# The third layer's expert steps, cut from 23 steps of 128 rows to 20 steps of two half blocks of 64 rows

## The reference, cut to what matters

```python
router_logits = x @ gate_weight.T                       # 1024 x 8
probs = softmax(router_logits); top_v, top_i = top_k(probs, 2)
top_v = top_v / top_v.sum(-1)
for each expert e:                                      # gate_up 1024 x 256, down 256 x 512
    gate, up = split(x @ gate_up[e].T)                  # 512 + 512 columns
    y_e = (silu(gate) * up) @ down[e].T                 # 256 columns
    out += weight_of_e_for_each_token * y_e
```

## Time and profile before

| | |
|---|---|
| median of 3 runs | 457.62 us |
| the three runs | 454.16, 457.62 and 458.86 us |
| span of the profiled execution | 455.4 us (its own device time is not given apart from the three runs) |
| PE busy | 407.7 us, 90% |
| first to last step of the third layer | from 249.21 us to 394.82 us of the span |

### The profile page before, as it was taken

The page is one execution under the profiler, slowest core; times in us unless marked ns, Lnnn a source line. Parts: engine busy times, 40 slices in busy tenths (PEclk is TensorE's granted clock), DMA queues, the critical chain, the costliest instruction groups (busy, mean ns, idle before and its releaser), DMA issues.

```text
span 455.4 us, 6054 instructions
## 1 busy us (share of the span) xinstructions
PE 407.7 (90%) x1749; PEld 265.4 (58%) x1749; DVE 328.5 (72%) x620; ACT 239.2 (53%) x478; POOL 253.2 (56%) x352
## 2 busy tenths in 40 slices
PE   7798999999899989957967999999999999976895
PEld 7576787555455545535753455566655566653554
DVE  5998789999999999799874466557546311038994
ACT  6533682667667667579853233232333232339883
POOL 5474037676879996137506457856864553214641
PEclk9999999999999999989965999999999999999998
DMA  7900006456555645000115987898898885050011
GB/s 230 411 11 0 1 1 221 138 185 224 184 158 191 212 163 184 1 1 2 39 55 178 376 299 280 304 374 299 305 361 300 285 317 192 35 184 1 23 35 37
DMA packets 23665, 77.39 MB, mean 170 GB/s; under 512 B 3441, under 2 KB 7921, under 8 KB 20177
## 3 DMA queue, kind: packets, MB, share of 16 engines
q1 hardware_dynamic: 20336, 69.94, 43.5%
q0 software_dynamic: 2208, 6.03, 4.1%
q10 hardware_dynamic: 1088, 1.05, 0.7%
HBM read 71.76 MB, written 5.24 MB: 169 GB/s over the span
## 4 chain that ended last, share of the span: by engine, by line
PE 50%; DVE 28%; issue 12%; ACT 3%; POOL 3%; DMA 3%; SPq 0%; DVEq 0%; POOLq 0%; ACTq 0%
PE bank L1993 18%; PE bank L2013 10%; PE bank L1770 5%; DVE hx L1295 4%; DVE fw L1084 4%; DVE bw L1087 3%; PE bank L1615 3%; PE bank L1617 2%; PE bank L1616 2%; DVE fw L1092 2%; PE bank L2004 2%; DVE xp L1353 2%; PE bank L1692 2%; DVE gl L1574 2%; PE bank L1839 1%
## 5 line engine op out<-in xcount | busy, mean ns | idle before, releaser
L1993 PE MATMUL bank<-gu,xbT 128*128 128x512 f32 x184 | 84.6, 603 | 0.9 <-ACT xbT L920 0.9
L1770 PE MATMUL bank<-hx,w2raw 128*128 128x512 f32 x128 | 67.3, 607 | 4.6 <-DVE hx L1295 3.7
L1510 DVE TENSOR_TENSOR hm<-bank,sl 128x512 f32<-128x512 f32 x23 | 15.9, 692 | 69.3 <-PE bank L1993 37.9
L808 ACT ACTIVATE rl<-bank 128x512 f32<-128x512 f32 x64 | 38.1, 595 | 38.6 <-PE bank L1617 37.8
L1993 PEld LDWEIGHTS bank<-gu,xbT 128*128 128x128 f32 x184 | 35.2, 194 | 36.3 <-issue 33.8
L1615 PE MATMUL bank<-xlhi,w1hi 128*128 128x512 f32 x64 | 49.4, 771 | 0.0
L2013 PE MATMUL bank<-dn,hT 128*128 128x256 f32 x184 | 45.2, 389 | 3.4 <-ACT hT L931 0.8
L589 POOL DMA_INDIRECT y_rows<-yb,dest_i x23 | 25.0, 1088 | 35.4 <-ACT yb L937 34.8
L1295 DVE TENSOR_TENSOR hx<-bank,cwb 128x512 f32<-128x512 f32 x64 | 42.1, 660 | 3.1 <-ACT bank L812 3.1
L2013 PEld LDWEIGHTS bank<-dn,hT 128*128 128x128 f32 x184 | 33.1, 190 | 11.8 <-issue 8.2
L1092 DVE RECIPROCAL fw<-fw 128x256 f32<-128x256 f32 x23 | 39.8, 1732 | 0.0
(11 more groups left out here) (305 smaller groups left out, 931.7 us busy)
## 6 DMA issues: line engine op xcount, KB each, us to landing
gu<-in_gu SPq DMA_DIRECT2D x22, 1024.0 KB, 7.6
cwb<-cw_rows SPq DMA_DIRECT2D x32, 512.0 KB, 4.1
dn<-in_dn SPq DMA_DIRECT2D x23, 512.0 KB, 4.5
traw<-in_t SPq DMA_DIRECT2D x3, 1024.0 KB, 7.5
w1raw<-in_w SPq DMA_DIRECT2D x8, 256.0 KB, 4.9
w2raw<-in_w SPq DMA_DIRECT2D x8, 256.0 KB, 4.6
kT<-in_kt SPq DMA_DIRECT2D x4, 256.0 KB, 4.5
x<-in_x SPq DMA_DIRECT2D x2, 512.0 KB, 6.4
```

What stands on the lines that cost most here:

```text
L808: act.activation(rl[:, u % 3, :], bank[u % 4][:], ACT.Relu).then_inc(sem("r_ready"), 1)
L1770: pe.matmul(bank[4 + s][:], w2raw[:, e // 4 % 2, e % 4, :], hx[:, 0, u % 4, :], start=(e == 0), stop=(e == E0 - 1), skip_group_check=True) ...
L1993: ins = pe.matmul(bank[2 * (b % 2) + up][:], xbT[:, b % 2, k, :], gu[:, b % RING, k, up * I2:up * I2 + I2], start=(k == 0), stop=(k == KC ...
```

## The change

A step now holds two half blocks of 64 rows, numbers 2b and 2b+1, each with an expert of its own. Experts get whole half blocks, of which 2048 pairs can need 39, so there are 20 steps. In gate_up and down each matmul becomes two: the first has the lower 64 columns of the stationary tile and writes PSUM partitions 0 to 63, the second the upper 64 and partitions 64 to 127, each with its own weights moving. `gu` and `dn` hold four buffers, two for each half, taken by the parity of b. A buffer is loaded again only if its new owner differs from the expert that it held two steps before; the DMA that is not needed is started with a false condition. All four buffers are first filled with expert 0 ahead of the routing. The waits on SP become: gate_up(b-2) done for `gu`, down(b-2) done for `dn`.

```diff
-NB = (TOP2 * TOK + E2 * (P - 1)) // P
-NBW = 24
+PART = 64
+GROUPS = P // PART
+NB = -(-((TOP2 * TOK + E2 * (PART - 1)) // PART) // GROUPS)
+NH = GROUPS * NB
+FULL = TOK // PART
+FIRST = [0] * GROUPS
...
-        gu = sb("gu", [P, RING, KC, 2 * I2])
-        dn = sb("dn", [P, RING, I2 // P, C])
+        gu = sb("gu", [P, 2 * GROUPS, KC, 2 * I2])
+        dn = sb("dn", [P, 2 * GROUPS, I2 // P, C])
...
+        def part(g):
+
+            return slice(PART * g, PART * g + PART)
...
             sp.dma_start(rtraw[:], rt_d).then_inc(sem("rt_in"), 16)
+            for slot in range(2 * GROUPS):
+                e = FIRST[slot // 2]
+                sp.dma_start(gu[:, slot, :, :], gu_d[e, :, :, :]).then_inc(sem(f"gu_in{slot % 2}"), 16)
+                sp.dma_start(dn[:, slot, :, :], dn_d[e, :, :, :]).then_inc(sem(f"dn_in{slot % 2}"), 16)
...
+            def owners(b):
+
+                for g in range(GROUPS):
+                    h = GROUPS * b + g
+                    owner[h] = sp.value_load(owner_i[h:h + 1, 0:1], min_val=0, max_val=E2 - 1)
+
+            def held(b, g):
+
+                return owner[GROUPS * (b - 2) + g] if b >= 2 else FIRST[g]
+
             def up_weights(b):
 
-                e = sp.value_load(owner_i[b:b + 1, 0:1], min_val=0, max_val=E2 - 1)
-                wait(sp, sem("up_done"), b - RING + 1)
-                sp.dma_start(gu[:, b % RING, :, :], gu_d[bass.ds(e, 1), :, :, :].rearrange("o p k n -> p (o k) n")
-                             ).then_inc(sem(f"gu_in{b % RING}"), 16)
...
+                wait(sp, sem("up_done"), b - 1)
+                if b < 2:
+                    sp.wait_ge(sem(f"gu_in{b}"), 16 * GROUPS)
+                for g in range(GROUPS):
+                    e, slot = owner[GROUPS * b + g], 2 * g + b % 2
+                    sp.dma_start(gu[:, slot, :, :], gu_d[bass.ds(e, 1), :, :, :].rearrange("o p k n -> p (o k) n"),
+                                 cond=e != held(b, g)).then_inc(sem(f"gu_in{slot % 2}"), 16)
 
             def down_weights(b):
 
-                e = sp.value_load(owner_i[b:b + 1, 0:1], min_val=0, max_val=E2 - 1)
-                wait(sp, sem("d_done"), b - RING + 1)
-                sp.dma_start(dn[:, b % RING, :, :], dn_d[bass.ds(e, 1), :, :, :].rearrange("o p k n -> p (o k) n")
-                             ).then_inc(sem(f"dn_in{b % RING}"), 16)
-
+                wait(sp, sem("d_done"), b - 1)
+                if b < 2:
+                    sp.wait_ge(sem(f"dn_in{b}"), 16 * GROUPS)
+                for g in range(GROUPS):
+                    e, slot = owner[GROUPS * b + g], 2 * g + b % 2
+                    sp.dma_start(dn[:, slot, :, :], dn_d[bass.ds(e, 1), :, :, :].rearrange("o p k n -> p (o k) n"),
+                                 cond=e != held(b, g)).then_inc(sem(f"dn_in{slot % 2}"), 16)
+
+            owner = {}
             sp.wait_ge(sem("owner_step"), 3)
...
-            for b in range(2, NB):
-                if b == 2:
-                    sp.wait_ge(sem("xb_in2"), 16)
+            for b in range(NB):
+                owners(b)
                 up_weights(b)
+                if b < 3:
+                    sp.wait_ge(sem(f"xb_in{b}"), 16)
                 down_weights(b)
                 if b in (8, 14):
                     ternary_in((1, 8, 14).index(b))
...
-                if b in (19, 20):
-                    combine_rows(b - 19)
+                if b in (17, 18):
+                    combine_rows(b - 17)
...
-            steps = r2c[:, 0, 0, :].rearrange("p (e j) -> p e j", j=E2)
-            chain(dve.tensor_tensor(steps, total.rearrange("p (e o) -> p e o", o=1).to_broadcast([P, E2, E2]),
-                                    edge[:].rearrange("p (o j) -> p o j", o=1).to_broadcast([P, E2, E2]), ALU.is_gt))
+            steps = r2c[:, 0, 0:2, :].rearrange("p a (e j) -> p (a e) j", j=FULL)
+            chain(dve.tensor_tensor(steps, total.rearrange("p (e o) -> p e o", o=1).to_broadcast([P, E2, FULL]),
+                                    edge[:].rearrange("p (o j) -> p o j", o=1).to_broadcast([P, E2, FULL]), ALU.is_gt))
...
-            first_of = starts[:, 1, 0:E2].rearrange("p (o e) -> p o e", o=1).to_broadcast([P, NT, E2])
+            chain(dve.tensor_scalar(starts[:, 0, 0:E2], starts[:, 1, 0:E2], 1.0 / GROUPS, None, ALU.mult))
+            first_of = starts[:, 0, 0:E2].rearrange("p (o e) -> p o e", o=1).to_broadcast([P, NT, E2])
...
                     for k in range(KC):
-                        ins = pe.matmul(bank[2 * (b % 2) + up][:], xbT[:, b % 2, k, :], gu[:, b % RING, k, up * I2:up * I2 + I2],
-                                        start=(k == 0), stop=(k == KC - 1))
+                        for g in range(GROUPS):
+                            ins = pe.matmul(bank[2 * (b % 2) + up][part(g), :], xbT[:, b % 2, k, part(g)],
+                                            gu[:, 2 * g + b % 2, k, up * I2:up * I2 + I2], start=(k == 0), stop=(k == KC - 1))
...
-                    ins = pe.matmul(y_bank(b), hT2[:, b % 2, j, :], dn[:, b % RING, j, :], start=(j == 0), stop=(j == 3))
+                    for g in range(GROUPS):
+                        ins = pe.matmul(y_bank(b)[part(g), :], hT2[:, b % 2, j, part(g)], dn[:, 2 * g + b % 2, j, :],
+                                        start=(j == 0), stop=(j == 3))
```

More of the change, by code:

```diff
@@ L41 @@
 TOP2 = 2
-NB = (TOP2 * TOK + E2 * (P - 1)) // P
-NBW = 24
+PART = 64
[4 more added lines that the diff above has]
+FIRST = [0] * GROUPS
 RING = 3
-HALVED = 1
 CRING = 4
@@ L140, in build @@
         part_no = sb("part_no", [P, 1])
-        slab = sb("slab", [P, NBW])
-        edge = sb("edge", [P, E2])
+        slab = sb("slab", [P, NB])
+        edge = sb("edge", [P, FULL])
         token_no = sb("token_no", [P, NT])
@@ L145, in build @@
         ones = sb("ones", [P, P])
-        slab_up = sb("slab_up", [P, NBW])
+        slab_up = sb("slab_up", [P, NB])
         starts = sb("starts", [P, 2, E2 + 1])
-        spare = sb("spare", [P, NBW])
+        spare = sb("spare", [P, NB])
         wmx = sb("wmx", [P, P])
@@ L189, in build @@
         lane_of = sb("lane_of", [P, 2 * NT, P], F16)
-        slab_of = sb("slab_of", [P, 2 * NT, NBW], F16)
-        slab_val = sb("slab_val", [P, 2 * NT, NBW], F16)
+        slab_of = sb("slab_of", [P, 2 * NT, NB], F16)
+        slab_val = sb("slab_val", [P, 2 * NT, NB], F16)
         r2c = sb("r2c", [P, 2, NT, E2 * E2], BF16)
@@ L215, in build @@
         owner_i = sb("owner_i", [P, 1], I32)
-        row_f = sb("row_f", [P, 4, NBW])
-        row_i = sb("row_i", [P, NBW], I32)
-        dest_i = sb("dest_i", [P, NBW], I32)
+        row_f = sb("row_f", [P, 4, NB])
+        row_i = sb("row_i", [P, NB], I32)
+        dest_i = sb("dest_i", [P, NB], I32)
         cw2p = sb("cw2p", [P, 2, NT])
@@ L368, in _ @@
                              cond[:, 2 * b:2 * b + 2, :]).then_inc(sem("rows_out"), 16)
-            def up_weights(b):
-                e = sp.value_load(owner_i[b:b + 1, 0:1], min_val=0, max_val=E2 - 1)
-                wait(sp, sem("up_done"), b - RING + 1)
-                sp.dma_start(gu[:, b % RING, :, :], gu_d[bass.ds(e, 1), :, :, :].rearrange("o p k n -> p (o k) n")
-                             ).then_inc(sem(f"gu_in{b % RING}"), 16)
-            def half_weights(b, up):
-                e = sp.value_load(owner_i[b:b + 1, 0:1], min_val=0, max_val=E2 - 1)
-                n = slice(up * I2, up * I2 + I2)
-                sp.dma_start(gu[:, b % RING, :, n], gu_d[bass.ds(e, 1), :, :, n].rearrange("o p k n -> p (o k) n")
-                             ).then_inc(sem(f"gu_in{b % RING}" if up else "half_in"), 16)
@@ L384, in down_weights @@
-            def down_weights(b):
-                e = sp.value_load(owner_i[b:b + 1, 0:1], min_val=0, max_val=E2 - 1)
-                wait(sp, sem("d_done"), b - RING + 1)
-                sp.dma_start(dn[:, b % RING, :, :], dn_d[bass.ds(e, 1), :, :, :].rearrange("o p k n -> p (o k) n")
-                             ).then_inc(sem(f"dn_in{b % RING}"), 16)
-            sp.wait_ge(sem("owner_step"), 3)
-            up_weights(0)
-            half_weights(HALVED, 0)
-            sp.wait_ge(sem("xb_in0"), 16)
@@ L447, in route_consts @@
                 pool.iota(lane[:], [[1, P]], base=0, channel_multiplier=0, **kw).then_inc(sem("route_consts"), 1)
-                pool.iota(slab[:], [[1, NBW]], base=0, channel_multiplier=0, **kw).then_inc(sem("route_consts"), 1)
-                pool.iota(edge[:], [[P, E2]], base=0, channel_multiplier=0, **kw).then_inc(sem("route_consts"), 1)
+                pool.iota(slab[:], [[1, NB]], base=0, channel_multiplier=0, **kw).then_inc(sem("route_consts"), 1)
+                pool.iota(edge[:], [[PART, FULL]], base=0, channel_multiplier=0, **kw).then_inc(sem("route_consts"), 1)
                 pool.iota(token_no[:], [[P, NT]], base=1, channel_multiplier=1, **kw).then_inc(sem("route_consts"), 1)
```

(21 more changed lines are left out.)

## The result

The changed kernel takes 493.17 us (median of 4 runs, 491.17 to 497.28) against 456.61 us (454.16 to 458.86). The ratio is 1.0815, with the interval 1.0751 to 1.0879: 8% slower. The forecast was 477, the range 439 to 500.

What follows compares the result with a forecast made beforehand. It took PE to bound the kernel before, DMA close behind, and transfers to bound the changed one. -18.5 + 8.0 + 29.9 (stalls) + 0.3 (routing) = +19.7 us on 457.62 gave 477, range 439 to 500.

Steps and rivals of the forecast that it cites:

- PE's side: On PE: three steps removed, -18.5 us; 20 steps each 0.4 us longer, +8.0 us.
- the stalls: Waits of PE for gu ahead of gate_up in the 20 steps: 29.9 us in all.
- The number of loads: Loads of gu and dn in steps 0 to 19: 27 pairs, against 23 in 23 steps before.
- The price of one weight load: On PE, loading weights of 64 columns: 136 ns each, adding 0.2 us a step in down.
- changes of form: On PE, two switches between 64-column and 128-column forms in each step: 0.1 us each, 0.2 a step.
- the list: Stalls step by step, from bytes between two gate_ups at 0.39 MB/us against a 6.6 us step: 29.9 us.
- the runs' first stalls: Steps 6, 10 and 17, beginning a run of loads with the queue empty: 3.4 us each, 10.2 in all.
- my 2.4: On SP: gu starts 2.4 us after the down product, behind two dn issues and two register loads.
- the 2.2: Fixed part of a gu transfer's landing time, besides movement of its bytes: 2.2 us.
- The clock: PE's clock could fall after stalls of 2 to 3.4 us: up to 1.8 us each, extending the range to 500.
- The distance: Between a gu's start on SP and its need on PE: one step, where three buffers gave two.
- they cancel: Rival for the whole kernel: 22 or 23 pairs, 0.42 MB/us, a step near 6.2 us: 453 to 462; chance 0.07.

Runs made afterwards that it cites:

- e1: Changed kernel with every gu and dn transfer of the 20 steps skipped, all instructions kept: 439.73 us, ratio 0.9628.
- e7: Kernel before the change, with two buffers for gu and dn instead of three: 498.94 us, ratio 1.0967.
- e2: Changed kernel with useless matmuls (fillers) on PE ahead of the wait for gu in eight steps: 490.78 us, ratio 1.0769.
- e3: Changed kernel with gu(b+1) started ahead of dn(b) in SP's list: 458.06 us, ratio 1.0024.
- e4: Changed kernel with half blocks 0 to 19 on the lower column half and 20 to 39 on the upper: 468.69 us, ratio 1.0277.
- e9: Changed kernel with the edits of e3 and e4 together, upper half's buffers filled ahead with expert 4: 442.62 us, ratio 0.9707.

## Why the prediction was right or wrong

**The mechanism was right**: the halves run together, PE's side gains, the loads bound the stage, and the kernel is slower. The sum was 20 us; measured are 36.6. The two terms that make up the sum were off in opposite directions, PE's side by 6.6 us and the stalls by 23.5, so that the total missed by no more than 17 us is in part luck.

**The number of loads** was right to the pair: 27 after the first four (42.47 MB over e1).

**PE's side** was priced too high: -18.5 + 8.0 + 0.3 = -10.2 against e1's -16.8, of which 1.5 is the quicker first gate_up. A step without loads took 6.32 us, under the 6.5 to 6.8 that I gave as the sign. The price of one weight load was right to the nanosecond, 136:

```profile
L2028 PEld LDWEIGHTS bank<-dn,hT 128*64 128x64 f32 x320 | 25.2, 136 | 12.4 <-issue 7.2
```

But 320 of them in a row would be 43.5 us, and they are busy for 25.2: the loads of the two halves overlap as the matmuls do, and nothing is added to a down pair (1.95 us for 16 records, where 1.97 were needed for 8). Of the two changes of form only one shows: the hidden transposes behind gate_up take 0.59 instead of 0.44.

**The stalls are the term that was mis-sized**: 29.9 against 53.4. Some of it is in the list itself: steps 6 and 17 have a dn of the step before in front (0.52 MB, 1.3 us each), and steps 6, 10 and 17 the 0.26 MB of gather and scatter (0.7 each), which the list leaves out, 4.7 us in all. (Two smaller slips change nothing: at 0.5 MB/us the runs' first stalls would be 2.2 us, not 1.9, and the list at 0.421 MB/us gives 28, not 27.) Three parts lie in the mechanism:
- Where. I let each step of a run stall by 2.1 us. In fact about every second one waits, by 2.4 to 5.3, since a stalled step lets the next load, already on its way, land. The sum of plain waits came near, 32.7.
- The landing. Inside a run of loads I let the queue run on without a break, 8.7 us for 3.41 MB. It doesn't: dn(b) is only let go by the down product, and at every second step of a run the weights' transfers have all landed by then (gu(2) at 265.66, dn(2) started at 267.26), so the start counts again. From down(0) to gate_up(3), 0.34 + 2.2 + 8.7 = 11.2 us, which is what was measured. SP needed 3.8 us until both gu were started (266.92 to 270.71), not the 2.7 that follow from my 2.4 and one more issue, since each conditional transfer has register instructions of its own; that mattered where no dn stood in front, as ahead of step 10, where the second gu was on its way 3.2 us after the down product. For one pair of dn and gu e7 shows 1.3 us more than the 2.2, at 0.39 MB/us.
- The clock. I named it, priced it at up to 1.8 us for each fall, and left it to the range. Eight falls cost 17.4 us in the trace. That would close the gap, and it is the tempting story; e2 says that it isn't an addend. With the clock held up the waits were 42.4 us and the median 2.4 us lower. Without the fillers' overrun some 39 us of waits are left, so that is, as an estimate, the right size of the stall term with a full clock, and the slow clock in part fills time that the transfers need anyway.

That waits and clock overlap is shown: 9.7 of the 15.7 us came back as waits, and up to 3.6 of them are the fillers' own. How the 53.4 us split between transfers and clock no run separates better than that.

**The distance** was named as what counts, and e7 and e3 show it as the cause: two ways to change it by one step or less, at equal bytes, move the time by 38 to 43 us and by 35. The rival "they cancel" was set at 22 or 23 pairs; e4 with 14 pairs still lost 2.8%, so the number of loads was never enough alone.

**The bandwidth figure** of the Trainium skill (DMA: Bandwidth & Descriptors, "Where 436 GB/s comes from"), about 358 GB/s for a core, was weighed and not used. e3 held 418 over 15 us, so for one core alone the measurement decides against it as a ceiling.

## What to carry to other kernels

Ask of each transfer not only whether its bytes fit beside the work, but how many steps lie between the event that lets it start and the instruction that needs it, and what stands ahead of it in its queue. A load with its wait long over that is listed behind one whose wait is not cost 35 us here, about as much as the missing buffer of e7; list them in the order in which they may start. Giving each half block its own expert paid here only when each half also kept its expert for several steps (e9 against e3): give each half its own consecutive run.

A stall on PE and the slow clock behind it are not to be added up before a run has held the clock.

## What the runs showed of the hardware

- Two float32 matmuls on 64 columns each take the time of one on 128 (3.43 us for 16 records of 512 columns, where the kernel before had 8; 6.87 with all 16 on one half), also with all four records of one half ahead of the other's in the source (3.45).
- Weight loads on two column halves overlap too: 320 loads of 136 ns were busy for 25.2 us.
- In the changed kernel the eight waits of PE from 2.4 to 5.3 us were each followed by a gate_up of 5.0 to 6.3 us (mean granted clock 0.69 in 273 to 284 us), those of 0.3 and 1.0 us by one of 3.65. The length of a wait alone doesn't decide it: 2.9 us in e9 and in step 11 of e4 left gate_up at 3.65, 2.2 in step 15 of e4 was followed by 5.35.
- The DMA engines held 418 GB/s for 15 us in e3, with both weights and gathers.
